# Layer 0 of a fused two-layer cross-attention kernel: the stack image written to DRAM straight from the turned context

## The reference

```
v, k = context by 16 heads of 8, times Wv, Wk ; q = layernorm(x) by heads, times Wq
energy = q . k                       # 16 heads, 56 x 1500 per batch
energy = where(mask == 0, -1e20, energy)
attn   = softmax(energy / sqrt(128))
x = x + tanh(g0) * ((attn @ v) @ Wo.T + bo)
x = x + tanh(g1) * (shared swiglu + the routed expert's swiglu)
```

## Time and profile before

| | |
|---|---|
| median of three runs | 1423.04 us (1422.51 to 1432.66) |
| the profiled execution | 1434.77 us, span 1433.0 us |
| TensorE (PE) busy | 1170.4 us (82%) |
| weight loads (PEld) | 687.9 us (48%) |
| VectorE (DVE) busy | 908.1 us (63%) |
| ScalarE (ACT) busy | 699.6 us (49%) |
| GpSimd (POOL) busy | 514.8 us (36%) |
| granted TensorE clock, mean | 0.862 |
| DMA | 172.25 MB, mean 120 GB/s |

### The profile page before, as it was taken

How to read it: one execution, slowest core, us unless ns; L and a number is a source line. 1 busy time by engine, 2 the same in 40 slices (tenths; PEclk the granted TensorE clock), 3 DMA queues, 4 the chain that set the end, 5 groups by cost and what they waited for, 6 DMA issues and landing times.

```text
span 1433.0 us, 29991 instructions
## 1 busy us (share of the span) xinstructions
PE 1170.4 (82%) x10822; PEld 687.9 (48%) x10824; DVE 908.1 (63%) x1533; ACT 699.6 (49%) x967; POOL 514.8 (36%) x350
## 2 busy tenths in 40 slices
PE   4556676777768766798878979999999999999984
PEld 1134444445445544556633435555555555555542
DVE  8544445555455444553587778777768776868777
ACT  2323333434334333334545656666666566656642
POOL 7242434443444444632433023222322232223220
PEclk9856778777677688757699999999999999999996
DMA  3435544444444444441000047767676666667640
GB/s 100 154 116 166 181 158 152 144 157 127 143 154 157 140 151 151 155 112 35 23 1 22 1 77 143 146 132 144 131 147 129 145 129 139 134 133 147 131 87 13
DMA packets 224346, 172.25 MB, mean 120 GB/s; under 512 B 183504, under 2 KB 195808, under 8 KB 222720
## 3 DMA queue, kind: packets, MB, share of 16 engines
q1 hardware_dynamic: 224000, 171.48, 47.0%
q10 hardware_dynamic: 288, 0.00, 0.0%
HBM read 100.37 MB, written 44.31 MB: 101 GB/s over the span
## 4 chain that ended last, share of the span: by engine, by line
PE 57%; DMA 17%; DVE 8%; issue 5%; ACT 5%; POOL 4%; SPq 4%; POOLq 0%; ACTq 0%; DVEq 0%; another core or an unknown queue 0%
PE bank L936 15%; PE bank L954 14%; DMA c_in<-in_ctx 11%; PE bank L904 5%; PE bank L852 4%; DMA turned_rows<-region 4%; SPq L409 4%; PE bank L821 3%; POOL region L664 3%; PE bank L826 2%; DVE region L1766 2%; PE bank L882 2%; PE bank L912 2%; ACT region L1338 2%; PE bank L1180 2%
## 5 line engine op out<-in xcount | busy, mean ns | idle before, releaser
L1582 DVE CUSTOM_DVE_ANT_0 e_row<-bank,region 120x1000 f32<-120x1000 f32 (+1 forms) x256 | 230.2, 937 | 270.6 <-PE bank L793 270.6
L1287 ACT ACTIVATE region<-bank 125x896 f32<-125x896 f32 x192 | 176.2, 917 | 238.3 <-PE bank L826 238.3
L1626 DVE TENSOR_REDUCE neg_max<-bank 128x1 f32<-128x1500 f32 x112 | 192.6, 1720 | 130.2 <-PE bank L936 130.1
L936 PE MATMUL bank<-region 128*128 128x500 f16 x1008 | 235.1, 379 | 3.2 <-ACT e_row L1314 1.8
L1323 ACT COPY region<-bank 128x768 f16<-128x768 f16 x224 | 177.8, 794 | 89.0 <-PE bank L904 89.0
L1314 ACT ACTIVATE e_row<-bank,neg_shift 128x1500 f32<-128x1500 f32 x112 | 169.2, 1511 | 68.1 <-DVE neg_shift L1630 38.6
L821 PE MATMUL bank<-row_of,region 56*128 56x448 bf16 x384 | 163.4, 425 | 14.9 <-ACT region L1287 6.8
L793 PE MATMUL bank<-region 49*128 49x500 f16 x384 | 138.9, 465 | 44.3 <-DVE part_max L1582 23.2
L826 PE MATMUL bank<-region 49*128 49x112 f16 x1536 | 166.3, 239 | 0.0
L612 POOL CAST u_w<-e_row 128x1500 f16<-128x1500 f32 x56 | 80.6, 1440 | 216.1 <-ACT e_row L1314 216.1
L612 POOL CAST wg_sb<-e_row 128x1500 f16<-128x1500 f32 x56 | 81.8, 1461 | 197.7 <-ACT e_row L1314 153.6
(11 more groups left out here) (219 smaller groups left out, 1663.0 us busy)
## 6 DMA issues: line engine op xcount, KB each, us to landing
region<-stack_rows SPq DMA_DIRECT2D x32, 588.0 KB
stack_rows<-turned_rows SPq DMA_DIRECT2D x96, 192.0 KB, 3.2
turned_rows<-region SPq DMA_DIRECT2D x16, 768.0 KB, 3.3
region<-turned_rows SPq DMA_DIRECT2D x32, 384.0 KB, 3.5
c_in<-in_ctx SPq DMA_DIRECT2D x16, 750.0 KB
split_rows<-region SPq DMA_DIRECT2D x16, 750.0 KB
e_row<-in_mask_Bx1xSxS_if SPq DMA_DIRECT2D x32, 328.1 KB
region<-split_rows SPq DMA_DIRECT2D x24, 250.0 KB
```

Source lines behind the costliest of these rows:

```text
L936: last = pe.matmul(score_banks1(par, t)[:, k, :], q1[:, ql, b, 128 * t:128 * (t + 1)], c_t1[par][:, cl, 4 * k:4 * k + 4, 0:KP], start=(ql ...
L1287: act.activation(p0[:, 2 * i:2 * i + 2, :], ring0("s", h, i)[0:KP, :, 0:HALF_ROWS], ACT.Exp, scale=SCALE0)\
L1582: dve.tensor_tensor_reduce(out=masked[:, 4 * KP * a:4 * KP * z].rearrange("p (a k) -> p a k", a=z - a), in0=bank[0:RT, a:z, 0:4 * KP], in1 ...
L1626: dve.tensor_reduce(neg_max[:, t:t + 1], score_banks1(par, t), AX.XY, ALU.max, negate=True)\
```

## The change

SP writes the image directly out of `c_t0` in SBUF to `stack_rows`, without reading `turned_rows` back. The image of a batch becomes two parts: n = 0 (high halves, four DMAs) after the first copy, n = 1 (low halves, two DMAs) after the second. In SP's queue the mask load moves ahead of `split_rows`, the context load of b + 3 stands between the two parts of the image, and `turned_rows` goes to the end. On TensorE the turns move to (1, 1) and (1, 3), with `RING0` to match. On GpSimd the mask of b + 1 goes ahead of the split of b + 2. ScalarE's copy into `c_t0` also waits for the image of the batch before.

```diff
-        PREP_AT = {(0, 3): 0, (1, 0): 1}
+        PREP_AT = {(1, 1): 0, (1, 3): 1}
...
-        def sync_image(sp, b, par):
-
-            wait_apart(sp, "sp", (sem("turned_out0"), 16 * (b + 1)))
-            if not (isinstance(b, int) and b < 2):
+        def sync_image(sp, b, par, n):
+
+            if n == 0 and not (isinstance(b, int) and b < 2):
                 for half in range(2):
                     wait_apart(sp, "sp", (sem(f"stack{par}_{half}"), per_use(b - 2, par, 32)))
-            turned = turned_rows[b].rearrange("(g p) n c k -> p n g (c k)", p=2 * D0)
-            for half in range(2):
-                for at, n in ((0, 0), (2 * D0, 1), (33, 0)):
-                    sp.dma_start(stack_rows[par, half, at:at + 2 * D0], turned[:, n, 4 * half:4 * half + 4])\
+            wait_apart(sp, "sp", (sem(f"ct_done0_{n}"), b + 1))
+            for at in ((0, 33), (2 * D0,))[n]:
+                for half in range(2):
+                    sp.dma_start(stack_rows[par, half, at:at + 2 * D0].rearrange("p g x -> g p x"),
+                                 c_t0[64 * half:64 * half + 64, n].rearrange("p c k -> p (c k)"))\
                         .then_inc(sem("image0"), 16)
...
                 if ahead > 2:
+                    sync_load_mask(sp, b + 2)
                     sync_split_out(sp, b + 2)
-                    sync_load_mask(sp, b + 2)
-                    sync_turned_out(sp, b + 2)
-                    sync_image(sp, b + 2, par)
+                    sync_image(sp, b + 2, par, 0)
                 if ahead > 3:
                     sync_load_context(sp, b + 3, 1 - par)
+                if ahead > 2:
+                    sync_image(sp, b + 2, par, 1)
+                    sync_turned_out(sp, b + 2)
...
             sync_split_out(sp, 0)
+            for n in range(2):
+                sync_image(sp, 0, 0, n)
             sync_turned_out(sp, 0)
             sync_load_mask(sp, 1)
             sync_split_out(sp, 1)
-            sync_image(sp, 0, 0)
             sync_stack(sp, 0, 0)
             sync_load_context(sp, 2, 0)
+            for n in range(2):
+                sync_image(sp, 1, 1, n)
             sync_turned_out(sp, 1)
-            sync_image(sp, 1, 1)
...
             def layer0(b, par, first, last):
+                if not last:
+                    mask0(b + 1, 1 - par)
                 if not (isinstance(b, int) and b + 2 >= B):
                     split0(b + 2, par)
-                if not last:
-                    mask0(b + 1, 1 - par)
...
                 act.wait_ge(sem("turned_out0"), 16 * b)
+                act.wait_ge(sem("image0"), 96 * b)
```

More of the change, by code:

```diff
@@ L288, in flamingo_kernel @@
         block = ctx.enter_context(nc.Block())
-        RING0 = [("s", 0, 0), ("s", 0, 1), ("spread", 0), ("s", 0, 2), ("s", 0, 3), ("prep", 0), ("s", 0, 4), ("s", 0, 5),
-                 ("neg", 0), ("s", 1, 0), ("prep", 1), ("s", 1, 1), ("spread", 1), ("s", 1, 2), ("s", 1, 3), ("s", 1, 4),
-                 ("s", 1, 5), ("neg", 1)]
-        PREP_AT = {(0, 3): 0, (1, 0): 1}
+        RING0 = [("s", 0, 0), ("s", 0, 1), ("spread", 0), ("s", 0, 2), ("s", 0, 3), ("s", 0, 4), ("s", 0, 5), ("neg", 0),
+                 ("s", 1, 0), ("s", 1, 1), ("prep", 0), ("spread", 1), ("s", 1, 2), ("s", 1, 3), ("prep", 1),
+                 ("s", 1, 4), ("s", 1, 5), ("neg", 1)]
+        PREP_AT = {(1, 1): 0, (1, 3): 1}
         ROWS_AT = (0, 1, 3, 4)
```

## The result

The changed kernel takes 1500.3 us (median of 4 runs, 1497.4 to 1515.7), the kernel before 1422.8 in the same comparison (4 runs, 1421.9 to 1432.7). The ratio is 1.055, with a 95% interval of 1.046 to 1.064. The forecast was 1438, within 1385 to 1500. The sign was right, the size far off: +78 us where +15 had been forecast. The profiled execution after has a span of 1495.6 us.

What follows compares the result with a forecast made beforehand. A wait sets the pace: a batch circle of 37.3 us through context load, split, turn and image. The new circle of 38.4 us over 13 periods adds 14 to 1423, giving 1437, stated as 1438; range 1385 to 1500.

Steps and rivals of the forecast that it cites:

- The width, 4 engines: New image DMAs from `c_t0`: four unjoined outer steps would spread each over 4 engines; the forecast's case, chance 0.70.
- the wide rival: Image DMAs stay on 16 engines: circle 30.6 us, 1332 us within 1315 to 1350; chance 0.18.
- 13 periods x (38.4 - 37.3) = +14 us: Layer 0, loads of batches 3 to 15: each period grows from 37.3 to 38.4 us; ends -14 and +39.
- the circle: Layer 0, per batch: stack landed, two slots, turn, copy, four image DMAs, context load, two image DMAs, stack load: 38.4 us.
- The last two periods have a lighter queue in both kernels: 0: Last two batch periods of layer 0: lighter DMA queue before and after, so no difference counted, 0 us.
- The first two batches: 0: First batches of layer 0: image of batch 0 starts some 3.3 us earlier but takes longer, so 0 taken.
- Mask ahead of split: free: GpSimd: the 6.54 us mask ahead of the split still ends before the turn needs it, so no cost.
- TensorE's rows wait for the stack load, 5 to 8 us in every batch: Sign of being right: TensorE's rows (L793) wait 5 to 8 us per batch for the stack load.
- Narrow and at the old pace: Slower rival: image on 4 engines at 18.4 KB/us each, period 42.9 us, 1495 us; chance 0.12.
- No gain or loss is taken: TensorE's mean clock of 0.72: one idle stretch per batch stays, so no time was added or removed.

Runs made afterwards that it cites:

- e2: The kernel before with only its six image DMAs rearranged to four outer steps on both sides, so four engines: 1502.9 us, 1.060.
- e9: The changed kernel with two added waits that hold GpSimd's mask and value copies until VectorE's neg step (`neg_max`, `none_valid`, `negc`) is over: 1495.4 us, 1.056.
- e10: The changed kernel's order, with the image gathered from `turned_rows` by the old 16-engine DMAs, all behind the context load: 1448.3 us, 1.021.
- e11: e10 with two added GpSimd waits on VectorE's neg step: 1418.7 us, 1.002.
- e6: The changed kernel without an image: `turned_rows` written straight from `c_t0`, the stack load gathering from it, mask still first: 1417.4 us, 0.999.
- e8: e6, mask kept first, with GpSimd's mask and value copies made to wait until VectorE's neg step is over: 1321.3 us, 0.935.
- e4: The changed kernel with the image in 24 DMAs of 16 partitions instead of 6, so each can use 16 engines: 1459.0 us, 1.029.
- e12: The kernel before with two added GpSimd waits on VectorE's neg step alone: 1404.7 us, 0.993.
- e3: The changed kernel with the context load behind both parts of the image in SP's queue instead of between them: 1506.1 us, 1.062.
- e5: e4 with GpSimd's mask put back behind the split: 1427.9 us, 1.007.

## Why the prediction was off

- **The width, 4 engines: right.** Shares of 0.22 to 0.28 behind the issues and 104 GB/s in after, 0.27 in e2, and e2 shows the price alone, +81 us (1502.9 against 1421.4). The Trainium skill's rule, DMA: Bandwidth & Descriptors, section "Why a DMA increments its semaphore by 16 and not by 1" (the slowest dimension of both sides counts), had spoken against the change, and the trace agrees. (Where the prediction says that counting only the SBUF side would give "the second rival's" sum, it means the wide rival, the first in its list.)
- **"13 periods x (38.4 - 37.3) = +14 us": the step that failed.** The 13 periods brought +61.1 us, 4.7 each and not 1.1. The sum priced every period as one in the middle of the loop. It missed in two places.
  - *In the loop* the circle was sized 38.4 us and measured 40.5 (40.2 with the collision taken away, e9), so +29.0 us over nine periods where the forecast had 9 x 1.1 = 10. The circle and its order were right. The batch shown, 39.9, misses 1.0 in the image with the context load, 0.1 in the stack load and 0.4 at the turn. The first 3 us of the image ran at 38 GB/s, not 102; that alone is 3 x (1 - 0.38) = 1.9 us, of which other pieces gave some back.
  - *Ahead of the loop*, the periods of batches 3 to 5 lost 27.7 us, 9.2 each. Weight loads of layer 0 stand in the same queue there (SP's issue of one, `sh_gate`, took 10.98 us after and 5.95 before), and the chain has the next two stack loads at 17.00 and 15.88 us, not 10.01. That fits a queue whose four busiest engines also carry the image. It is read from the traces, not tried: what the weight loads cost by themselves was not measured.
- **"The last two periods have a lighter queue in both kernels: 0": failed too.** They brought +16.5 us. Their queue is lighter, but their images must still land ahead of the stack loads. Which piece cost how much was not measured. "The first two batches: 0" held as far as it can be seen: batch 2's context load is issued at 57.7 us, before at 58.0.
- **"Mask ahead of split: free": false as a statement.** The prediction asked what stands behind the mask on GpSimd and not what runs beside it. It makes `none_valid` 3.8 us long, and the wait for the neg step is 65.4 of the 87 us that TensorE waits. In the changed kernel's time this hides behind the queue (e9: 5 us, within the noise). With a wide or no image, keeping the neg step apart is worth 30 to 96 us (e10 with e11, e6 with e8). No rival named it, though the earlier trace rows had the 6.54 us operation and the chain of before the 5.22 us step quoted above.
- **"TensorE's rows wait for the stack load, 5 to 8 us in every batch": half right.** 21.6 us in 7 waits, since the collision took the rest. With it gone they are 90.7 us in 10 waits (e9), 9.1 each.
- **The rivals.** Wide: false for this DMA, but e8 shows its period of 30.2 us was to be had. "Narrow and at the old pace": its time, 1495, was close, its mechanism false (25 KB/us an engine and more, not 18.4, in after and e2). A near number for a wrong reason.
- **Clock.** "No gain or loss is taken": the mean clock of a batch is 0.60 against 0.72. Whether this adds to the loss or only follows from the idle time was not separated.

## What to carry to other kernels

Before costing a DMA whose two sides are ordered differently, write down the outer dimension of both sides as the instruction carries it; if the common divisor is small, cost the DMA, and everything behind it in its queue, at that few engines, in the first and last batches too, where other loads share the queue or the cover is thinner. When an operation of GpSimd moves, look which small VectorE operations with two SBUF inputs it will start beside: what it waits for may come at the same moment of every batch as what they wait for. And take away both of two near-equal circles before judging a change by its time: here the guard alone gave 5 us on the changed kernel, the direct path alone 83, and both 179, which made the kernel 6.5% faster than before.

## What the runs showed of the hardware

- A VectorE operation on 120x1 elements takes 0.16 us alone and 5.24 us in the chain of e4 beside GpSimd's 6.5 us operation over 120x1500. Two added waits that keep such operations apart gave 0.7% in before (e12), 2% in e11 and 6 to 7% in e8 (against e10 and e6).
- The same image bytes on four engines rather than 16 cost 81 us in the kernel before (e2), at 25 to 26 KB/us an engine.
- Moving the context load within its queue, from ahead of the image's last part to behind it, but still ahead of the stack load, saved nothing: e3 took 5.4 us off the image's landing and put 6.5 on the stack load's.
- The narrow image of after starts at 38 GB/s for some 3 us and later holds 100. Which part of it (descriptors, the writes of SP's next issues, the partition order) is the cause stays open. What bounds e5 and e11 at 35 to 36 us a period is, by their waits, the stack load; no kernel took that away and kept the image.
